# Planning a fused four-stage convolution kernel by half layers: exponentials and joins over two PSUM banks at once

## The chip, the cores and the metric

The kernel runs on one core of one Trainium2 chip. The metric is the device time of one execution in microseconds (us), the median of three. PE is TensorE, PEld its weight load, ACT ScalarE, DVE VectorE, POOL GpSimd, SP the engine that issues most DMAs. "Granted clock" is the share of TensorE's full 2.4 GHz that the throttle granted.

## The reference, cut to what matters

Input `x` is (8, 16, 128, 128) float32. Four residual stages follow each other, each on a group-normalised copy (8 groups, so 2 channels per group):

```python
x = x + _L0_conv_ref(_gn(x), ...)   # 3x3 conv, kernel mixed from 3 experts by a softmax routing of the pooled input
x = x + _L1_conv_ref(_gn(x), ...)   # abs, then depthwise 3x3
x = x + _L2_conv_ref(_gn(x), 8)     # 17 x 17 box mean, separable
x = x + _L3_conv_ref(_gn(x), ...)   # sum of 8 neighbours, then 1x1 layers:
h = elu(w1 n); h = elu(w2 h); h = elu(w3 h); h = elu(w4 h); F = w5 h   # 64 hidden channels
```

The last stage costs most: four layers of 64 x 64 products over 16,384 pixels per sample, each followed by `elu(z) = max(z, exp(min(z, 0)) - 1)`.

## The kernel before, in words

A sample lies in SBUF as 128 partitions (16 channels x 8 rows of a group of rows) x 2048 elements, cut into Q = 4 parts of 512. The first three stages (called k = 0, 1, 2) of one sample are interleaved by hand with the last stage (k = 3) of an earlier one. A round t (`one(t)`, t = 1 to 8, in each engine's block) computes the 16 layers (4 parts x 4 layers) of sample t-1's last stage, the box stage of sample t, the second convolution of sample t+1 and parts of the first one and of the statistics of samples t+1 to t+3. Before t = 1 stands a prologue. In the plan `at` = 0 to 15 counts the layers of a round, and each engine's `one(t)` says which other piece it does after which layer. Each engine runs its instructions in this order; semaphores join them.

One layer works on M = 4 PSUM banks `pz[:, m, :]` (128 x 512). Per bank (lines 785 to 801, 650 to 672, 1017 to 1043 of the kernel):

- PE (`layer`) waits for bank m of the previous layer's result (`g_written`), then multiplies: two 64 x 64 tiles, each in two float32 passes, so four matmul instructions. Even banks use the diagonal quadrants of the array, odd banks the other two, so two neighbouring banks can run at once.
- ACT (`elu`) computes `u = relu(-z)` from PSUM (L654), then `u = exp(-u)` in place (L662). It issues relu 0, relu 1, exp 0, relu 2, exp 1, relu 3, exp 2, exp 3: no exponential follows its own relu directly.
- DVE (`join`, L1025) computes `g = max(u - 1, z)`, and the next layer's matmul of that bank can go.

After a part's fourth layer PE multiplies by w5 into bank `po` (`last_layer`, L807) and DVE adds it to the sample (`output`, L1047). For the last sample, and for the first part of the one before, DVE has little else to do: there `clips` gives it banks 1 and 3, where it writes `min(z, 0)` itself (L1021) in place of ACT's relu, and ACT applies exp to that (L659); in the last sample the join of bank 3 is carried over into the next layer's time.

The other pieces that the plan places: `conv_taps` (PE, L777) 16 matmul instructions on 64 x 32 tiles for one column of taps; `box_band` (PE, L746) two instructions on the whole array, 12 bands per sample, into `pc` (`chunk_bank`); `box_scan` (DVE, L1058); `evacuate` (DVE, L1008, L1011, L1013) adds a stage's result to the sample; `chunk_stats` and `merge_stats` (DVE, L967 to L975), then `group_sums` (PE, L720), `group_var` (DVE, L982) and `scales` (POOL, L467 to L477) make a normalisation; `normal1` (ACT, L642) writes the second stage's input in two halves of 1024, `normal0` (L628 on ACT in the prologue, POOL afterwards) the first stage's, `normal2` (POOL, L525) the third's and `normal3` (DVE, L1065) the fourth's; `near_sums` (POOL) and `stacks` (DMAs, SP) prepare the fourth stage's operand, `windows0` and `windows1` (DMAs, SP) those of the first two.

Of the kernel before, what the change touches and what calls it, by code (L numbers as in the profile page):

```python
# [21 lines left out]
Q = 4  # L22
# [53 lines left out]
def build(nc, x, w_experts, conv_bias, fc_w, fc_b, w_depth, w1, w2, w3, w4, w5, con_early, con_channel, con_late, out):  # L76
    with ExitStack() as ctx:
# [122 lines left out]
        clip_done = sem("clip_done")  # L200
# [36 lines left out]
        Y0 = 8  # L237

# [9 lines left out]
        def carried(j, q):  # L248

            return isinstance(j, int) and j == B - 1 and q < Q - 1  # L250

        def steps(j, q, l, m, counted):

            n = sum(LAYERS * len(counted(i, p)) for i in range(j + 1) for p in range(Q) if (i, p) < (j, q))
            c = counted(j, q)
            return n + l * len(c) + c.index(m) + 1

        def clip_n(j, q, l, m):

            return steps(j, q, l, m, clips)  # L260

        def relu_n(j, q, l, m):

            if not isinstance(j, int):
                return zn(j, q, l, m)
            return steps(j, q, l, m, lambda i, p: [a for a in range(M) if a not in clips(i, p)])

        def elus(l):

            return g_last if l == LAYERS - 1 else g  # L270

# [78 lines left out]
        def windows1(eng, i, halves, last):  # L350

            for h in halves:
                eng.wait_ge(y1_written, 2 * i + h + 1)
                for dst, rows in around(y1, win1, h, False):
                    eng.dma_start(dst, rows).then_inc(win1_in, 16)
            if last:
                eng.wait_ge(y1_written, 2 * i + 2)
# [91 lines left out]
        def _(pool):  # L449
# [14 lines left out]
            def scales(i, k):  # L464
# [7 lines left out]
                if k < 2 and not (isinstance(i, int) and i == 0):  # L472
                    pool.wait_ge((y0_written, y1_written)[k], (Y0, 2)[k] * i)
# [82 lines left out]
            def one(t):  # L556
                if has(t + 1):
                    scales(t + 1, 1)
# [11 lines left out]
                if has(t + 3):  # L570
                    scales(t + 3, 0)
                    pool_features(t + 3)
# [24 lines left out]
            scales(3, 0)  # L597
            pool_features(3)
# [7 lines left out]
        def _(act):  # L606
# [29 lines left out]
            def normal1(i, half):  # L636
                if half == 0:
# [3 lines left out]
                rows = slice(half * K // 2, (half + 1) * K // 2)  # L641
                act.activation(y1[:, rows, 1:W + 1], sample(i).rearrange("p (k w) -> p k w", w=W)[:, rows, :], ACT.Abs,  # L642
# [7 lines left out]
            def elu(j, q, l):  # L650

                def relu(m):
# [3 lines left out]
                def exp(m):  # L656
                    if m in clips(j, q):
                        act.wait_ge(clip_done, clip_n(j, q, l, m))
                        act.activation(u[:, m, :], u[:, m, :], ACT.Exp).then_inc(exp_done, 1)  # L659
                    else:  # L660
                        act.wait_ge(relu_done, relu_n(j, q, l, m))
                        act.activation(u[:, m, :], u[:, m, :], ACT.Exp, scale=-1.0).then_inc(exp_done, 1)  # L662

                if clips(j, q):
                    relu(0)
                    exp(0)
                    exp(1)
                    relu(2)
                    exp(2)
                    exp(3)  # L670
                else:
                    relu(0)
                    for m in range(1, M):
                        relu(m)
                        exp(m - 1)
                    exp(M - 1)

            def one(t):
                first = isinstance(t, int) and t == 1
                for p in range(4):  # L680
                    for l in range(LAYERS):
                        at = 4 * p + l
                        elu(t - 1, p, l)
                        if has(t + 1):
                            if at - first in (4, 5):
                                normal1(t + 1, at - first - 4)
                        if has(t + 2):
                            if at == 5 + first:
                                softmax_exp(t + 2)
# [5 lines left out]
            normal1(0, 0)  # L695
            normal1(0, 1)
# [9 lines left out]
            normal1(1, 0)  # L706
            normal1(1, 1)
# [7 lines left out]
        def _(pe):  # L715
# [15 lines left out]
            def box_band(i, c, d):  # L731
                if d == 0:
                    if isinstance(i, int) and i == 0:
                        pe.wait_ge(conv_evac[0], Q + max(c - 1, 0))
                    elif c >= 2:
                        pe.wait_ge(conv_evac[2], Q * i + c - 1)
# [14 lines left out]
            def conv_taps(i, k, n, taps):  # L751

                if taps[0] == 0:
# [6 lines left out]
                    elif k == 1:  # L760
                        if isinstance(i, int) and i == 0:
                            pe.wait_ge(setup_dve, SETUP_DVE)
                        else:
                            pe.wait_ge(conv_evac[2], Q * i)
# [17 lines left out]
            def layer(j, q, l):  # L782
                top, bottom = slice(0, HID), slice(HID, P)
                for m in range(M):
# [20 lines left out]

# [4 lines left out]

            def one(t):
                first = isinstance(t, int) and t == 1
                for p in range(4):
                    for l in range(LAYERS):
                        at = 4 * p + l
                        layer(t - 1, p, l)
                        if l == 0 and part_before(t, p):
                            last_layer(*part_before(t, p))
                        if has(t):
                            if at == 2:  # L820
                                box_band(t, 0, 0)
                                box_band(t, 0, 1)
                            if at == 3:
                                box_band(t, 0, 2)
                                box_band(t, 1, 0)
                            if at == 4:
                                box_band(t, 1, 1)
                            if at == 5:
                                box_band(t, 1, 2)
                                box_band(t, 2, 0)  # L830
                            if at == 6:
                                box_band(t, 2, 1)
                                box_band(t, 2, 2)
                            if at == 7:
                                box_band(t, 3, 0)
                                box_band(t, 3, 1)
                            if at == 8:
                                box_band(t, 3, 2)
                        if has(t + 1):
                            if first and at < 2:  # L840
                                conv_taps(t + 1, 0, at, range(3))
                            elif at == 0:
                                conv_taps(t + 1, 0, 1, (2,))
                            if at == 9:
                                conv_taps(t + 1, 1, 0, (0, 1))
                            if at == 10:
                                conv_taps(t + 1, 1, 0, (2,))
                            if at == 11:
                                conv_taps(t + 1, 1, 1, (0, 1))
                            if at == 12:  # L850
                                conv_taps(t + 1, 1, 1, (2,))
                        if has(t + 2):
                            if at == 13:
                                conv_taps(t + 2, 0, 0, (0, 1))
                            if at == 14:
                                conv_taps(t + 2, 0, 0, (2,))
                            if at == 15:
                                conv_taps(t + 2, 0, 1, (0, 1))
                        if at == 3 + first and has(t + 1):
                            group_sums(t + 1, 1)  # L860
                        if at == 4 + first and has(t + 2):
                            logits(t + 2, (t + 1, 1))
                        if at == 9 and has(t):
                            group_sums(t, 3)
                        if at == 10 and has(t + 3):
                            group_sums(t + 3, 0)
                        if at == 14 and has(t + 1):
                            group_sums(t + 1, 2)
# [39 lines left out]
            group_sums(3, 0)  # L908
# [8 lines left out]
        def _(dve):  # L917
# [99 lines left out]
            def elu(j, q, l):  # L1017

                def clip(m):
                    dve.wait_ge(z_mm, zn(j, q, l, m))  # L1020
                    dve.tensor_scalar(u[:, m, :], pz[:, m, :], 0.0, None, ALU.min).then_inc(clip_done, 1)  # L1021

                def join(l, m, q=q):
                    dve.wait_ge(exp_done, zn(j, q, l, m))
                    dve.scalar_tensor_tensor(out=elus(l)[:, m, :], in0=u[:, m, :], scalar=-1.0, in1=pz[:, m, :],  # L1025
                                             op0=ALU.add, op1=ALU.max).then_inc(g_written, 1)

# [246 lines left out]
```

## Time and profile before

| | us |
|---|---|
| time, median of 3 runs (lowest, highest) | 763.07 (761.76, 764.73) |
| the profiled execution: its own time | 764.65 |
| its span, first to last instruction | 762.8 |
| PE busy in the span | 616.3 (81%) |
| DVE busy | 596.9 (78%) |
| ACT busy | 548.8 (72%) |
| POOL busy | 265.8 (35%) |

The span begins with about 141 us of prologue. The eight rounds follow, and about 14 us of last output and store. Busy time of an engine is the union of its instructions' durations; in a stretch of back-to-back instructions these overlap at their ends, so the distance from one start to the next (the step) is shorter than a duration. The profile was taken at a granted clock of 0.953 on average.

### The profile page before, as it was taken

How to read it: one execution, taken by the hardware profiler on the slowest of the kernel's cores; microseconds unless marked ns; L12 is line 12 of the kernel's file. 1: busy time of each engine (PE TensorE's matmuls, PEld its weight loads, DVE VectorE, ACT ScalarE, POOL GpSimd, SP SyncE). 2: the span in 40 equal slices, each digit the busy share in tenths (PEclk: the TensorE clock that was granted, in tenths of full speed). 3: DMA queues.
4: the chain of work that ended last, by engine and by line, in shares of the span. 5: the costliest groups of instructions: out<-in, count | busy, mean ns of one | idle time of the engine just before them, and what ended most of it. 6: DMA issues, size and time to landing. Idle time of an engine off the chain costs nothing.

```text
span 762.8 us, 13243 instructions
## 1 busy us (share of the span) xinstructions
PE 616.3 (81%) x4142; PEld 186.8 (24%) x4142; DVE 596.9 (78%) x1020; ACT 548.8 (72%) x1041; POOL 265.8 (35%) x431
## 2 busy tenths in 40 slices
PE   0352844789988999899989988999899789899992
PEld 0211211123223232222223322322222223222220
DVE  1242675399988998899899989878887889779993
ACT  0212110489988988898889888988898968998882
POOL 1314025407551656155624552455211620230000
PEclk9985887799999999999999999999999999999996
DMA  5749589608685858272926383646540650075002
GB/s 100 133 86 170 123 174 205 104 1 173 143 193 96 195 117 197 55 179 50 200 68 157 66 187 89 136 88 154 123 112 1 139 137 1 1 154 122 1 1 55
DMA packets 72866, 85.53 MB, mean 112 GB/s; under 512 B 8674, under 2 KB 58354, under 8 KB 72818
## 3 DMA queue, kind: packets, MB, share of 16 engines
q1 hardware_dynamic: 68096, 78.58, 47.8%
q10 hardware_dynamic: 4722, 6.34, 4.7%
q8 instruction: 26, 0.43, 0.3%
q14 instruction: 22, 0.18, 0.1%
HBM read 9.14 MB, written 8.39 MB: 23 GB/s over the span
## 4 chain that ended last, share of the span: by engine, by line
PE 33%; DVE 22%; ACT 19%; issue 10%; DMA 7%; SPq 5%; POOL 1%; ACTq 1%; DVEq 0%; POOLq 0%
PE pz L800 16%; ACT u L654 8%; ACT u L662 7%; PE pc L746 7%; PE pc L777 7%; DVE g L1025 6%; DMA win<-y 3%; DVE u L1021 3%; ACT u L659 2%; DVE bn L967 2%; DVE box_sum L1058 2%; DVE xs L1008 2%; DMA xs<-in_x_dram 2%; DVE g_last L1025 2%; SPq L375 1%
## 5 line engine op out<-in xcount | busy, mean ns | idle before, releaser
L654 ACT ACTIVATE u<-pz 128x512 f32<-128x512 f32 x472 | 275.1, 600 | 96.2 <-PE pz L800 95.4
L800 PE MATMUL pz<-g,wT 64*64 64x512 f32 x1536 | 288.1, 607 | 19.6 <-DVE g L1025 16.3
L1025 DVE SCALAR_TENSOR_TENSOR g<-u,pz 128x512 f32<-128x512 f32 x384 | 250.5, 682 | 61.7 <-ACT u L662 58.9
L662 ACT ACTIVATE u<-u 128x512 f32<-128x512 f32 x472 | 288.1, 639 | 1.3
L800 PEld LDWEIGHTS pz<-g,wT 64*64 64x64 f32 x1536 | 78.4, 131 | 206.3 <-issue 204.3
L777 PE MATMUL pc<-win,t 64*32 64x512 f32 x1392 | 95.5, 651 | 22.3 <-DMA win<-y 13.5
L746 PE MATMUL pc<-box_sum,box_mat 128*128 128x512 f32 x180 | 92.5, 631 | 12.3 <-DVE box_sum L1058 12.3
L967 DVE BATCH_NORM_STATS2 bn<-xs 128x6 f32<-128x512 f32 (+1 forms) x128 | 82.7, 681 | 19.0 <-DMA xs<-in_x_dram 17.2
L800 PE MATMUL pz<-stack,wT 64*64 64x512 f32 x512 | 83.8, 620 | 10.0 <-issue 5.5
L1025 DVE SCALAR_TENSOR_TENSOR g_last<-u,pz 128x512 f32<-128x512 f32 x128 | 82.7, 681 | 10.3 <-ACT u L662 9.1
L467 POOL TENSOR_TENSOR stat<-stat 128x1 f32<-128x1 f32 x32 | 11.1, 348 | 227.2 <-DVE stat L982 227.2
L720 PE MATMUL psm<-stat,con 128*128 128x2 f32 x64 | 12.4, 264 | 55.3 <-DVE stat L975 52.1
L642 ACT ACTIVATE y<-xs,stat 128x1024 f32<-128x1024 f32 (+1 forms) x16 | 19.9, 1258 | 44.5 <-POOL stat L477 44.5
L746 PEld LDWEIGHTS pc<-box_sum,box_mat 128*128 128x128 f32 x180 | 30.2, 189 | 73.2 <-issue 47.0
L777 PEld LDWEIGHTS pc<-win,t 64*32 64x32 f32 x1392 | 24.1, 112 | 86.4 <-issue 86.4
L1058 DVE TENSOR_TENSOR_SCAN box_sum<-y 128x580 f32<-128x580 f32 x32 | 43.1, 1354 | 1.6 <-DMA stack<-near_sum 1.6
L550 POOL TENSOR_TENSOR near_sum<-box_sum 128x512 f32<-128x512 f32 x30 | 31.8, 1060 | 36.0 <-DVE box_sum L1065 36.0
L800 PEld LDWEIGHTS pz<-stack,wT 64*64 64x64 f32 x512 | 24.2, 134 | 62.4 <-issue 60.3
L554 POOL TENSOR_TENSOR near_sum<-near_sum,box_sum 128x512 f32<-128x512 f32 x30 | 37.7, 1258 | 4.3 <-DVE near_sum L1086 2.0
L807 PE MATMUL po<-g_last,w5T 128*32 128x512 f32 x256 | 35.0, 619 | 2.8 <-DVE g_last L1025 2.8
L525 POOL TENSOR_TENSOR y<-xs,stat 128x512 f32<-128x512 f32 x20 | 20.8, 1042 | 42.4 <-DVE box_sum L1058 42.4
L659 ACT ACTIVATE u<-u 128x512 f32<-128x512 f32 x40 | 25.2, 629 | 12.2 <-DVE u L1021 12.0
(91 smaller groups left out, 413.8 us busy)
## 6 DMA issues: line engine op xcount, KB each, us to landing
stack<-near_sum SPq DMA_DIRECT2D x90, 192.0 KB, 4.0
win<-y SPq DMA_DIRECT2D x56, 260.0 KB, 4.2
win<-y SPq DMA_DIRECT2D x56, 195.0 KB, 4.3
out_dram<-xs SPq DMA_DIRECT2D x8, 1024.0 KB
stack<-box_sum SPq DMA_DIRECT2D x60, 128.0 KB, 3.9
xs<-in_x_dram SPq DMA_DIRECT2D x7, 1024.0 KB
stack<-near_sum SPq DMA_DIRECT2D x30, 128.0 KB, 2.9
win<-y ACTq DMA_DIRECT2D x8, 260.0 KB, 6.8
```

The source lines that it names most:

```text
L550: pool.tensor_tensor(o, y[:, :, 0:W], y[:, :, 1:W + 1], ALU.add).then_inc(near_pairs_done, 1)
L554: pool.tensor_tensor(o, o, y[:, :, 2:W + 2], ALU.add).then_inc(near_rows, 1)
L654: act.activation(u[:, m, :], pz[:, m, :], ACT.Relu, scale=-1.0, bias=0.0).then_inc(relu_done, 1)
L659: act.activation(u[:, m, :], u[:, m, :], ACT.Exp).then_inc(exp_done, 1)
L662: act.activation(u[:, m, :], u[:, m, :], ACT.Exp, scale=-1.0).then_inc(exp_done, 1)
L746: mm = pe.matmul(chunk_bank(i, c), box_mat[:, d, :], box_sum[:, c * KB + d:(c + 1) * KB + d, RAD:RAD + W], start=d == 0, stop=d == 2)
L777: last = pe.matmul(pair_banks(i, k, n)[2 * C * m:2 * C * m + 2 * C, h, :], mat[rows, kw, :], blocks(win[m // 2], n + 2 * h)[rows, :, kw:kw ...
L800: last = pe.matmul(pz[to, m, :], wT[rows, l, rows], src, start=True, stop=True)
L807: last = pe.matmul(po[32 * m:32 * m + 32, :], w5T[:, :], elus(LAYERS - 1)[:, m, :], start=True, stop=True)
L967: dve.bn_stats(bn[k][:, c, :], sample(i, c)).then_inc(stat_step[k], 1)
L1025: dve.scalar_tensor_tensor(out=elus(l)[:, m, :], in0=u[:, m, :], scalar=-1.0, in1=pz[:, m, :], op0=ALU.add, op1=ALU.max).then_inc(g_writte ...
L1058: dve.tensor_tensor_scan(own_rows(box_sum, c).rearrange("p k w -> p (k w)"), y2[:, c * n + BOX:(c + 1) * n + BOX], y2[:, c * n:(c + 1) * n ...
```

## The change

The unit of the plan becomes the half layer (32 slots `at` per round, `HALVES = 2 * LAYERS`), in which banks 2a and 2a+1 are worked on together. ACT does two single relus, then waits for both and does one exponential over the two banks (128 x 1024); DVE does one join over the two. `clips` and `carried` go, with DVE's `min` in the tail: all samples run alike. `normal1` comes in four pieces of 512 in place of two of 1024. The statistics' end, `group_sums`, `group_var`, `scales` and `pool_features` of sample t+2's first stage move from the end of the round before to the start of round t (POOL does them first). Box chunk 3 goes into `po` in place of `pc`, with new waits for `out_evac` before it and, for part 1, for `conv_evac[2]` before `last_layer`; `last_layer` moves off the first half layer for some parts. All other pieces are laid out anew over the 32 slots.

```diff
+        Y1 = 4
+        HALVES = 2 * LAYERS
-        def clips(j, q):
-            return (1, 3) if isinstance(j, int) and (j == B - 1 or j == B - 2 and q == 0) else ()
...
+        def pair_of(t, a):
+            return t[:, 2 * a:2 * a + 2, :].rearrange("p m n -> p (m n)")
-            return pc[:, c % 2, :]
+            return po[:, :] if c == Q - 1 else pc[:, c % 2, :]
...   (POOL, one(t))
+                if has(t + 2):
+                    scales(t + 2, 0)
+                    pool_features(t + 2)
                 if has(t + 1):
                     scales(t + 1, 1)
...
-                if has(t + 3):
-                    scales(t + 3, 0)
-                    pool_features(t + 3)
...   (ACT)
+            def normal1(i, c):
+                if c == 0:
                     act.wait_ge(norm_step[1], i * NORM + NORM)
...
+                act.activation(blocks(y1, c)[:, :, 1:W + 1], sample(i, c)..., ACT.Abs,
                                bias=st[1][:, 1:2], scale=st[1][:, 0:1]).then_inc(y1_written, 1)
+            def elu(j, q, l, a):
+                for m in (2 * a, 2 * a + 1):
                     act.wait_ge(z_mm, zn(j, q, l, m))
                     act.activation(u[:, m, :], pz[:, m, :], ACT.Relu, scale=-1.0, bias=0.0).then_inc(relu_done, 1)
+                act.wait_ge(relu_done, zn(j, q, l, 2 * a + 1))
+                act.activation(pair_of(u, a), pair_of(u, a), ACT.Exp, scale=-1.0).then_inc(exp_done, 2)
...
+                            elu(t - 1, p, l, a)
+                            if has(t + 1) and at - 3 * first in (5, 6, 7, 8):
+                                normal1(t + 1, at - 3 * first - 5)
+                            if has(t + 2) and at == 13:
                                 softmax_exp(t + 2)
...   (PE)
+            def layer(j, q, l, a):
+                for m in (2 * a, 2 * a + 1):
...
+                if q == 1 and has(j + 1):
+                    pe.wait_ge(conv_evac[2], Q * (j + 1) + Q)
...
+            box_at = {5: ((0, 0),), 6: ((0, 1),), 7: ((0, 2), (1, 0)), 8: ((1, 1),), 10: ((1, 2),), 11: ((2, 0),),
+                      12: ((2, 1),), 13: ((2, 2),), 14: ((3, 0),), 15: ((3, 1), (3, 2))}
+            last_at = {1: 0, 9: 1, 19: 2, 25: 3}
+            taps1_at = {16: (0, 0), 17: (0, 1), 18: (0, 2), 20: (1, 0), 21: (1, 1), 22: (1, 2)}
+            taps0_at = {24: (0, 0), 26: (0, 1), 27: (0, 2), 29: (1, 0), 30: (1, 1), 31: (1, 2)}
...
+                            if has(t + 2) and at == 0:
+                                group_sums(t + 2, 0, (t, 2))
+                            if has(t + 1) and at == 3 + 3 * first:
+                                group_sums(t + 1, 1)
...   (DVE)
+            def join(j, q, l, a):
+                dve.wait_ge(exp_done, zn(j, q, l, 2 * a + 1))
+                dve.scalar_tensor_tensor(out=pair_of(elus(l), a), in0=pair_of(u, a), scalar=-1.0, in1=pair_of(pz, a),
+                                         op0=ALU.add, op1=ALU.max).then_inc(g_written, 2)
+            output_at = {1: 0, 10: 1, 20: 2, 26: 3}
...
+                            if has(t + 3):
+                                if at in (17, 25, 29, 30):
+                                    chunk_stats(t + 3, 0, (17, 25, 29, 30).index(at))
+                                if at == 30:
+                                    merge_stats(t + 3, 0)
+            def near_stage(i, at):
+                if at in (3, 5, 7, 9):
+                    box_scan(i, (at - 3) // 2)
+                if at in (8, 11, 13, 15):
+                    evacuate(i, 2, (8, 11, 13, 15).index(at))
+                if at in (8, 11, 13, 16):
+                    chunk_stats(i, 3, (8, 11, 13, 16).index(at))
+                if at == 16:
+                    merge_stats(i, 3)
+                if at == 18:
+                    group_var(i, 3)
+                if at in (20, 21):
+                    normal3(i, at - 20)
+            def next_stage(i, at, first):       # the branch for t > 1
+                    if at == 0:
+                        stats_of(i, 1, (1, 3))
+                    if at == 1:
+                        merge_stats(i, 1)
+                    if at == 3:
+                        group_var(i, 1)
+                if at in (18, 22):
+                    evacuate_pair(i, 1, (at - 18) // 4)
+                if at == 19:
+                    chunk_stats(i, 2, 0)
+                if at == 23:
+                    stats_of(i, 2, (2, 1))
+                if at == 24:
+                    chunk_stats(i, 2, 3)
+                    merge_stats(i, 2)
+                if at == 26:
+                    group_var(i, 2)
+            def full_stage(i, at):
+                if at == 0:
+                    group_var(i, 0)
+                if at == 12:
+                    softmax_in(i)
+                if at == 14:
+                    route_out(i)
+                if at in (27, 31):
+                    evacuate_pair(i, 0, (at - 27) // 4)
+                if at == 28:
+                    stats_of(i, 1, (0, 2))
```

## Rows read from the trace of the kernel before

**Rows 1.** The page, parts 1 and 4: busy time, the chain that ended last.

```profile
PE 616.3 (81%) x4142; PEld 186.8 (24%) x4142; DVE 596.9 (78%) x1020; ACT 548.8 (72%) x1041; POOL 265.8 (35%) x431
PE 33%; DVE 22%; ACT 19%; issue 10%; DMA 7%; SPq 5%; POOL 1%; ACTq 1%; DVEq 0%; POOLq 0%
```

**Rows 2.** Windows by round: start:end, us, busy (x) by engine, clock, DMA, GB/s.

```profile
141.00:221.30 80.30, 75.87 (x592) 22.83 (x588) 70.36 (x120) 68.54 (x132) 34.45 (x56) 0.98 0.55 115
221.30:533.80 312.50, 289.89 (x2065) 87.83 (x2060) 278.30 (x466) 274.39 (x529) 149.28 (x227) 1.00 0.58 128
533.80:609.30 75.50, 67.74 (x432) 20.35 (x426) 64.04 (x105) 68.38 (x130) 22.25 (x31) 1.00 0.40 93
609.30:683.30 74.00, 66.16 (x316) 18.23 (x310) 59.99 (x93) 63.45 (x121) 16.81 (x21) 0.98 0.31 70
683.30:748.40 65.10, 59.65 (x282) 13.54 (x280) 62.34 (x101) 56.33 (x96) 0.00 (x0) 1.00 0.19 45
```

**Rows 3.** Waits of ACT from 200 to 600 us: engine line waited for, total us, times, longest.

```profile
ACT u L654 <- PE pz L800: 47.8, 49, 1.5
```

**Rows 4.** Groups by line and shape: xcount | busy us, mean ns | idle before, releaser.

```profile
L628 ACT ACTIVATE y<-xs,stat 128x512 f32<-128x512 f32 x12 | 9.1, 804 | 20.6 <-DMA win<-y 10.4 <-POOL stat L477 10.2
L642 ACT ACTIVATE y<-xs,stat 128x1024 f32<-128x1024 f32 x10 | 12.3, 1253 | 44.5 <-POOL stat L477 44.5
L1065 DVE TENSOR_SCALAR box_sum<-xs,stat 128x1024 f32<-128x1024 f32 x10 | 8.0, 805 | 1.9 <-POOL stat L477 1.9
L1065 DVE TENSOR_SCALAR box_sum<-xs,stat 128x1024 f32 x6 | 7.7, 1290 | 0.0
```

**Rows 5.** Timeline, start of round 3: start us, us, instruction, xcount, [idle <-releaser].

```profile
299.74 1.09 ACT L654 ACTIVATE u<-pz 128x512 f32<-128x512 f32 x2 [1.23 <-PE pz L800]
300.71 0.63 ACT L662 ACTIVATE u<-u 128x512 f32<-128x512 f32 x1
301.37 0.69 DVE L1025 SCALAR_TENSOR_TENSOR g<-u,pz 128x512 f32<-128x512 f32 x1 [0.87 <-ACT u L662]
301.49 1.09 PE L777 MATMUL pc<-win,t 64*32 64x512 f32 x16
303.74 1.18 ACT L654 ACTIVATE u<-pz 128x512 f32<-128x512 f32 x2
...
310.76 1.26 DVE L1025 SCALAR_TENSOR_TENSOR g<-u,pz 128x512 f32<-128x512 f32 x2
310.90 2.00 PE L746 MATMUL pc<-box_sum,box_mat 128*128 128x512 f32 x4 [0.70 <-DVE box_sum L1058]
...
312.82 1.95 PE L800 MATMUL pz<-g,wT 64*64 64x512 f32 x16
313.94 1.08 ACT L654 ACTIVATE u<-pz 128x512 f32<-128x512 f32 x2 [1.27 <-PE pz L800]
```

**Rows 6.** Timeline of the last round, about 742 us.

```profile
741.74 1.47 DVE L1025 SCALAR_TENSOR_TENSOR g<-u,pz 128x512 f32<-128x512 f32 x2
742.39 0.58 ACT L654 ACTIVATE u<-pz 128x512 f32<-128x512 f32 x1
743.00 0.63 ACT L662 ACTIVATE u<-u 128x512 f32<-128x512 f32 x1
743.32 0.22 PEld L800 LDWEIGHTS pz<-g,wT 64*64 64x64 f32 x4 [0.56 <-issue]
744.37 0.58 ACT L654 ACTIVATE u<-pz 128x512 f32<-128x512 f32 x1
```

**Rows 7.** Timeline of round 7, the scan of its first part.

```profile
619.03 1.37 DVE L1058 TENSOR_TENSOR_SCAN box_sum<-y 128x580 f32<-128x580 f32 x1 [1.56 <-DMA stack<-near_sum]
621.61 0.63 ACT L659 ACTIVATE u<-u 128x512 f32<-128x512 f32 x1 [2.92 <-DVE u L1021]
```

**Rows 8.** Windows in the prologue, PE's busy time against the clock (columns as rows 2).

```profile
104.00:110.00 6.00, 2.65 (x8) 1.00 (x6) 3.13 (x7) 2.37 (x2) 1.75 (x8) 1.00 0.42 95
116.00:124.00 8.00, 3.57 (x36) 1.65 (x44) 4.37 (x10) 0.00 (x0) 7.33 (x12) 0.50 1.08 197
```

More of the change, by code:

```diff
@@ L681, in one @@
                     for l in range(LAYERS):
[L682 to L688, printed above, removed]
+                        for a in range(2):
+                            at = HALVES * p + 2 * l + a
+                            elu(t - 1, p, l, a)
+                            if has(t + 1) and at - 3 * first in (5, 6, 7, 8):
+                                normal1(t + 1, at - 3 * first - 5)
+                            if has(t + 2) and at == 13:
                                 softmax_exp(t + 2)
@@ L694, in _ @@
             windows0(act, 0, (1,), False)
-            normal1(0, 0)
-            normal1(0, 1)
+            for c in range(Q):
+                normal1(0, c)
             windows1(act, 0, (1,), False)
@@ L705, in _ @@
                 normal0(2, c)
-            normal1(1, 0)
-            normal1(1, 1)
+            for c in range(Q):
+                normal1(1, c)
             act.wait_ge(conv_mm[1], 2)
@@ L839, in one @@
[L839 to L862, printed above, removed]
@@ L1164, in one @@
-                        if has(t + 3):
-                            if at == 7:
-                                chunk_stats(t + 3, 0, 0)
-                                chunk_stats(t + 3, 0, 1)
-                                chunk_stats(t + 3, 0, 2)
-                            if at == 9:
-                                chunk_stats(t + 3, 0, 3)
-                                merge_stats(t + 3, 0)
-                            if at == 12:
-                                group_var(t + 3, 0)
+                        for a in range(2):
+                            at = HALVES * p + 2 * l + a
+                            join(t - 1, p, l, a)
+                            near_stage(t, at)
+                            next_stage(t + 1, at, first)
+                            full_stage(t + 2, at)
+                            if at in output_at and part_before(t, output_at[at]):
+                                output(*part_before(t, output_at[at]))
+                            if has(t + 3):
[3 more added lines that the diff above has]
+                                    merge_stats(t + 3, 0)
@@ new lines, in near_stage @@
+            def near_stage(i, at):
+                if not has(i):
+                    return
+                if at in (3, 5, 7, 9):
[10 more added lines that the diff above has]
+                    normal3(i, at - 20)
@@ L1175, in evacuate_pair @@
+            def full_stage(i, at):
+                if not has(i):
+                    return
+                if at == 0:
[8 more added lines that the diff above has]
+                    stats_of(i, 1, (0, 2))
             def evacuate_pair(i, k, n):
@@ L1238, in _ @@
             merge_stats(3, 0)
-            group_var(3, 0)
             evacuate_pair(1, 1, 0)
```

220 lines of the change are left out of this document (45 added, 175 removed).

## The prediction

> **What bounds the kernel now.** I read the page first, then windows by round, the waits of ACT, the groups by shape, and two timelines. No engine is full: PE 81%, DVE 78%, ACT 72%, and the chain that ended last changes hands all the time (PE 33%, DVE 22%, ACT 19%) [rows 1]. Rounds 2 to 5 together take 312.5 us, 78.1 each, with PE busy for 72.5 of them, DVE 69.6 and ACT 68.6; the last round takes 65.1 [rows 2]. ACT's only long wait is for the next layer's product: 47.8 us in 400, in 49 pieces of about 1 us [rows 3]. So two things alternate. A layer with nothing beside it takes 4.0 us (its first relu starts at 299.74, the next layer's at 303.74 [rows 5]), which is eight ACT instructions at a mean of 0.50 us from start to start. A loaded layer is paced by the loop exp, join, matmul, relu with another piece in its way: there the reader is to see ACT idle 1.27 us before 313.94, after a scan on DVE (1.37 us long in [rows 7]) and four box instructions on PE (2.00) held up the joins and the products [rows 5]. The mean is 78.1 / 16 = 4.88 us a layer in a full round, 4.07 in the last.
>
> **Step 1: the new loop.** A half layer of the new plan can't start before the same half of the layer before is joined, and every instruction in it now waits for the whole of the one before. Link by link:
> - two single relus: 1.08 us (the pair at 313.94 [rows 5]);
> - the exponential now follows its own relu, which nothing did before outside the tail. A relu of 0.58 us starts at 742.39 and the exp that waits for it at 743.00, so 0.03 us between end and start [rows 6]. The drain that a back-to-back pair hides (two relus take 1.08 us, so the second starts 0.48 after the first, which lasts 0.60 [rows 5]) is in the open, 0.15 with the wait;
> - the exponential of 128 x 1024, not in the trace. One of 512 takes 0.63 [rows 5, 6]. ACT's other instruction takes 1.253 for 1024 and 0.804 for 512, 0.45 more [rows 4], which makes 1.08; from above it is two steps as now, 0.63 + 0.53 = 1.16. The 512 form of that row ran in the prologue only and reads short rows, so I put the difference a little lower and take 1.05, with 1.02 as the low end;
> - from its end to the join 0.03 us (301.34 to 301.37 [rows 5]);
> - the join of 128 x 1024, not in the trace either. From above 1.26 to 1.29: two joins back to back [rows 5], and the slow form of the DVE copy of 1024; from below that copy's fast form, 0.81 [rows 4]. A join reads two tensors, one of them in PSUM, so its own row is nearest. The 0.57 that a second join adds holds some fixed time, which one instruction pays once; I take 0.04 off, 1.22;
> - from the end of a join to the next relu: 743.21 to 744.37 is 1.16 us for one bank, of which about 0.14 until PE starts (its weights come at 743.32) [rows 6]; for two banks at once 312.82 to 313.94, 1.12 [rows 5]. Together 0.14 + 1.12 = 1.26.
>
> Sum: 1.08 + 0.03 + 1.05 + 0.03 + 1.22 + 1.26 = 4.67 us a layer. The two halves run in turn, so a slot is 2.335 us. That is more than ACT's own work: 0.48 + 0.60 + 0.03 until the exp starts and about 0.94 for its step (0.10 less than its duration) is 2.05 a slot, 4.10 a layer, and that in turn is no less than the 4.0 of now: the pairing saves a fixed part of about 0.1 per exponential and pays 0.15 for the drain in front of it. A round is at least 16 x 4.67 = 74.7 us. The bounds (exp 1.02 to 1.16, join 0.81 to 1.29) give 4.23 to 4.85.
>
> On the exponential the Trainium skill, in "ScalarE: Activation LUTs", *What ACT_TABLE_LOAD costs*, has a formula: with constant scale and bias 186 ns plus 0.833 ns per element, and about 93 ns of overlap between neighbours. Its 0.61 us for 512 stands against 0.63 here, and for 1024 it gives an estimate of 1.04 us; with that the loop would be 4.66.
>
> **Step 2: what hides beside it in a full round.** A slot leaves PE 2.335 - 1.0 (two banks dense: 16 instructions in 1.95 us for four banks [rows 5]) = 1.3 us and DVE 2.335 - 1.13 = 1.2 us. One box band (2.00 / 2) or one column of taps (1.09) fits [rows 5]; of DVE's pieces of 512, which I all take at the 0.6 us of a join's step, one fits and two nearly. So the stalls of rows 5 are gone: products no longer sit behind two bands, and PE doesn't stagger its banks. What doesn't fit:
> - normal1 on ACT: four slots (5 to 8) of 2.05 + 0.70 (0.804 less the overlap of 0.10 [rows 4]) = 2.75, 0.42 over each: 1.7 us. The two halves of now cost 2 x 1.15 us. The scales that it waits for come from `group_var` in slot 3, which lies behind a scan; POOL then has some 2 us, as now.
> - PE, slots 7 and 15: two bands, 1.0 + 2.0 = 3.0. Slot 7 hides under normal1, 15 counts 0.5.
> - DVE, slot 20: join, normal3 (1.29), output (0.60) is 3.0: 0.5 counted, as relief in the slots before takes the rest. Slots 27, 31 and 0 (pairs of evacuations or statistics, 1.4 us beside the join): 0.2 each, 0.5 in all after the light slot 30.
> - Scans (1.37 [rows 7]) and the evacuation with its statistics are 0.1 to 0.15 over in slots 3, 5, 7, 8, 9, 11 and 13. An excess after one half pushes only the other one, and two in a row of the same half cost once, so I count nothing; counted in full it is 0.8.
> - POOL's moved `scales` and `pool_features`, SP's windows and stacks: each has several slots (over 10 us) before its reader, as now; the waits for `po` (slots 14 and 19) come after the output of slot 10 and the evacuation of slot 15. Nothing; if one were late it would cost its lateness once a round.
>
> A full round: 74.7 + 1.7 + 1.5 = 77.9. That is 0.2 less than now: the half-layer plan hides nearly all the extra work, under a loop that is as long as what it hides.
>
> **Step 3: the rounds without that work.** From round 6 on there is less and less to hide, and the loop stays. Round 6 loses slots 27 and 31: 74.7 + 1.7 + 1.1 = 77.5 against 75.5 [rows 2]. Round 7 has no normal1: 74.7 + 1.1 = 75.8 against 74.0, although a stall there, in which the scan waits 1.56 us for a stack's DMAs and ACT then 2.92 us [rows 7], should go: normal3 is one or two slots earlier in the plan. The last round: 74.7 us and 0.5 for the longer last join, against 65.1 to 65.2. Without clips ACT takes back two relus a layer, but that isn't what costs: the clips let DVE and ACT share a bank's chain, and with single banks half a layer takes 1.98 us (742.39 to 744.37 [rows 6]). The pair can't go below its own chain, 4.67.
>
> **The sum.** Rounds 2 to 5: 4 x 77.9 = 311.6 against 312.5 [rows 2]: -0.9. Round 1 is 80.3 now [rows 2]; 74.7 + 1.7 + 1.7 (its evacuations crowd slots 0 to 5) + 0.5 + 1.5 (first stack) is 80.1: 0. Round 6 +2.0, round 7 +1.8, round 8 +10.0. Prologue: one `group_var` less, four pieces of normal1 in place of two on the way to the first windows, 0. Together +12.9: 764.65 of the profiled execution becomes 777.6. That execution lay 1.6 above the median of 763.07; between 776.0 and 777.6 I say 777.
>
> **The rivals.**
> - *Collisions in the full rounds* (chance 0.15). Every excess counted in full (0.8 and 1.2 more of slots 7, 20 and 27 to 0), and normal1 waiting 0.5 for its scales: 80.4 a round, 2.5 more in five rounds, 2 in round 6 and 1.5 in round 7: 777 + 16 = 793. For it: waits on a pair are longer than on one bank, so each delay holds 1024 elements. Against: phases of the halves may shift.
> - *The clock falls in the last round* (0.12). Products now come in bursts of 1.1 us every 2.335, PE busy for 47%, against 59.65 / 65.1 = 92% now, with its banks staggered [rows 2]. In the prologue the clock stayed at 2.4 GHz over a stretch with 2.65 of 6 us busy (44%) and was at 1.2 GHz in one with 3.57 of 8 (45%) [rows 8]. At 1.2 GHz a burst of 1.1 us takes about 0.85 longer (its columns take twice the time): 16 x 0.85 = 14 us, 791. The Trainium skill, "TensorE: Matmul & The Clock Gate", *A second HAM failure mode: psum-queue depth-cycling*, says that frequent short idles between groups of matmuls can make the clock swing between its two levels; the full rounds of now, with PE at 92%, show none of it.
> - *The relief wins* (0.07, the other side). Place: the full rounds; mechanism: dense PE pairs and cheap pair joins. With a loop of 4.60 and none of the heavy slots of DVE and PE showing, a full round is 73.6 + 1.7 = 75.3: -2.8 in each of four rounds, -3 in round 1, then -0.6 in rounds 6 and 7 together and +9 in the last, -6 in all: 763 - 6 = 757. It decides once a full round is under 76.4, since five of them must give back the last rounds' 8.4. With the join near its low end of 0.81 it goes to about 745, where the engines' own work would hold it. Against it: the join would have to leave its own row.
> - *It comes out even* (0.08): full rounds near 76.5, the tail as I say, 760 to 766.
>
> **How the numbers follow.** The forecast, 770 to 785, has 0.58. Slower: 0.58 + 0.15 + 0.12 = 0.85; within 0.5%, which is about what a measurement tells here, 0.08; faster 0.07. The range leaves out the faster rival, the even one and the top of the two slow ones: 767 to 792.
>
> **What would show it.** Right: exp groups of 1.05 us, joins of 1.22, layers of 4.67 in the last round with ACT idle about 0.6 a layer before its relus and released by PE, full rounds of 77 to 79, last round 74 to 76. Wrong: a last round under 72 (a link of the loop is shorter than I have it), full rounds off by over 2 us either way, ACT or DVE waiting for POOL or a DMA in each round, or a clock under 1.00 after 200 us.

## The result: 815.4 us, 6.7% slower

The changed kernel takes 815.38 us (median of 4, 814.38 to 816.6) against 763.9 of the kernel before: ratio 1.067, 95% interval 1.0625 to 1.0715. I had forecast slower, 777 us, and a range up to 792. The direction was right, the size a quarter of what came: +13 forecast, +51 measured. The time is above the range.

The profiled execution of the changed kernel took 814.6 us, span 812.8. Its page, parts 1 and 2, and the groups of the three instructions of the loop and of the relu (columns as in [rows 4]):

```profile
PE 594.2 (73%) x4142; PEld 173.5 (21%) x4142; DVE 555.1 (68%) x724; ACT 580.1 (71%) x841; POOL 261.8 (32%) x431
PEclk9975977999999999999999999999996998988765
L631 ACT ACTIVATE u<-pz 128x512 f32<-128x512 f32 x512 | 276.8, 592 | 102.5 <-PE pz L758 98.3
L633 ACT ACTIVATE u<-u 128x1024 f32<-128x1024 f32 x256 | 270.6, 1057 | 23.7 <-ACT u L631 0.4
L958 DVE SCALAR_TENSOR_TENSOR g<-u,pz 128x1024 f32<-128x1024 f32 x192 | 233.9, 1218 | 120.9 <-ACT u L633 120.0
```

Every engine is less busy than in [rows 1] except ACT, and the span is longer: the kernel waits more. The wide exponential (over two banks) takes 1.057 us and the wide join 1.218, as taken (1.05, 1.22). What is new is ACT's 23.7 us of idle time in front of the wide exponential, 0.09 for each of 256, and a clock that no longer stays up at the end. Of the 50 us between the two profiled spans, 48.5 lie in the eight rounds. Rounds 1, 2, 4, 6, 7 and 8 (columns as in [rows 2]):

```profile
141.70:225.30 83.60, 72.31 (x604) 20.12 (x604) 68.62 (x89) 70.82 (x102) 41.05 (x62) 0.99 0.60 121
225.30:308.50 83.20, 72.53 (x518) 21.59 (x516) 67.65 (x87) 71.13 (x102) 37.11 (x58) 0.98 0.66 140
389.00:468.80 79.80, 70.78 (x519) 21.41 (x517) 67.49 (x87) 71.05 (x103) 37.12 (x58) 1.00 0.54 120
548.90:631.40 82.50, 66.15 (x416) 17.59 (x414) 61.82 (x72) 70.57 (x101) 21.53 (x30) 0.92 0.43 97
631.40:711.80 80.40, 58.79 (x317) 16.29 (x314) 53.51 (x53) 68.07 (x96) 10.70 (x14) 0.94 0.28 64
711.80:797.60 85.80, 56.52 (x282) 13.05 (x280) 41.48 (x36) 67.92 (x97) 0.00 (x0) 0.75 0.06 15
```

Round 4 takes 79.8 us (78.3 before). Rounds 3 and 5 take 80.5 and 80.1, each with one fall of the clock, and round 2 takes 83.2 with one slow layer (e9 and e10 below). The last round takes 85.8 at a mean clock of 0.75, where [rows 2] had 65.1 at 1.00. The last round holds nothing but the layers, and it is the longest.

The loop itself, from the timeline of round 4, links one after another:

```profile
437.28 1.07 PE L767 MATMUL po<-g_last,w5T 128*32 128x512 f32 x8
437.34 1.09 ACT L631 ACTIVATE u<-pz 128x512 f32<-128x512 f32 x2 [0.33 <-PE pz L758]
438.48 1.29 PE L758 MATMUL pz<-g,wT 64*64 64x512 f32 x8
438.52 1.06 ACT L633 ACTIVATE u<-u 128x1024 f32<-128x1024 f32 x1
439.68 1.22 DVE L958 SCALAR_TENSOR_TENSOR g<-u,pz 128x1024 f32<-128x1024 f32 x1
441.05 1.29 PE L758 MATMUL pz<-g,wT 64*64 64x512 f32 x8 [0.21 <-DVE g L958]
```

Two relus 1.09 (437.34 to 438.43), 0.09 to the exponential, 1.06, 0.10 to the join (439.58 to 439.68), 1.22, 0.15 to PE at 441.05, and the relu of the next layer came at 442.16, 1.11 later: 4.82 us. My sum had 4.67: every link agrees to 0.01 but the two starts of a wide instruction, 0.09 and 0.10 in place of 0.03. In the second half of round 4 the layers follow each other at 4.82 to 5.02 us, whatever lies beside them (a w5 product at 437.28 here). In its first half, where the box bands, the scans and normal1 lie, most take 4.94 to 5.64.

The clock's part can be read in the last round. Two pairs of neighbouring layers, one of each at full clock and one with a fall to the lower level (0.50):

```profile
738.10:742.90 4.80, 2.39 (x18) 0.70 (x16) 3.03 (x4) 4.17 (x6) 0.00 (x0) 1.00 0.00 0
742.90:748.60 5.70, 4.34 (x18) 1.04 (x16) 2.43 (x3) 4.28 (x6) 0.00 (x0) 0.57 0.01 3
765.20:770.00 4.80, 2.28 (x16) 0.70 (x16) 2.66 (x4) 4.17 (x6) 0.00 (x0) 1.00 0.00 0
770.10:775.80 5.70, 4.18 (x17) 0.89 (x16) 2.43 (x3) 4.27 (x7) 0.00 (x0) 0.58 0.01 3
```

With the same layer to do, PE is busy 4.2 to 4.3 us in place of 2.3 to 2.4, and the layer takes 0.9 longer. Of the 16 layers of that round six take 4.82, and the ten that take 5.1 to 6.3 all have a mean clock under 1.00.

### The profile page after: what moved, and what is told of

The parts are those of the page before. It is cut to its first block, busy times and chain, and to the rows that moved or that the text cites. A ratio compares the mean times of both kernels' runs of the same rounds, so it can differ in the third digit from the quotient of the medians.

```text
span 812.8 us, 13218 instructions
## 1 busy us (share of the span) xinstructions
PE 594.2 (73%) x4142; PEld 173.5 (21%) x4142; DVE 555.1 (68%) x724; ACT 580.1 (71%) x841; POOL 261.8 (32%) x431
## 4 chain that ended last, share of the span: by engine, by line
PE 27%; ACT 23%; DVE 19%; issue 16%; DMA 5%; POOL 4%; SPq 2%; ACTq 1%; DVEq 0%; POOLq 0%
PE pz L758 16%; ACT u L631 11%; ACT u L633 10%; DVE g L958 9%; PE pc L735 4%; DMA win<-y 3%; DVE g_last L958 2%; SPq L335 2%; PE po L704 2%; DVE bn L905 2%; ACT y L619 2%; PE po L767 2%; DMA xs<-in_x_dram 2%; PE pc L704 2%; POOL y L494 2%
## 5 line engine op out<-in xcount | busy, mean ns | idle before, releaser
L758 PE MATMUL pz<-g,wT 64*64 64x512 f32 x1536 | 255.9, 659 | 85.3 <-DVE g L958 82.2
L958 DVE SCALAR_TENSOR_TENSOR g<-u,pz 128x1024 f32<-128x1024 f32 x192 | 233.9, 1218 | 120.9 <-ACT u L633 120.0
L633 ACT ACTIVATE u<-u 128x1024 f32<-128x1024 f32 x256 | 270.6, 1057 | 23.7 <-ACT u L631 0.4
L735 PE MATMUL pc<-win,t 64*32 64x512 f32 x1392 | 101.0, 657 | 29.9 <-DMA win<-y 15.6
L958 DVE SCALAR_TENSOR_TENSOR g_last<-u,pz 128x1024 f32<-128x1024 f32 x64 | 78.0, 1218 | 43.1 <-ACT u L633 42.7
L447 POOL TENSOR_TENSOR stat<-stat 128x1 f32<-128x1 f32 x32 | 6.2, 193 | 214.8 <-DVE stat L920 214.8
L704 PE MATMUL pc<-box_sum,box_mat 128*128 128x512 f32 x138 | 74.6, 635 | 0.2
L619 ACT ACTIVATE y<-xs,stat 128x512 f32<-128x512 f32 (+1 forms) x32 | 25.1, 801 | 46.6 <-POOL stat L457 46.6
L704 PEld LDWEIGHTS pc<-box_sum,box_mat 128*128 128x128 f32 x138 | 21.5, 188 | 52.4 <-issue 43.8
L496 POOL TENSOR_TENSOR y<-y,stat 128x512 f32<-128x512 f32 x28 | 29.2, 1043 | 2.2
```

Source lines behind the costliest of these rows:

```text
L619: act.activation(blocks(y1, c)[:, :, 1:W + 1], sample(i, c).rearrange("p (k w) -> p k w", w=W), ACT.Abs, bias=st[1][:, 1:2], scale=st[1][: ...
L633: act.activation(pair_of(u, a), pair_of(u, a), ACT.Exp, scale=-1.0).then_inc(exp_done, 2)
L704: mm = pe.matmul(chunk_bank(i, c), box_mat[:, d, :], box_sum[:, c * KB + d:(c + 1) * KB + d, RAD:RAD + W], start=d == 0, stop=d == 2)
L735: last = pe.matmul(pair_banks(i, k, n)[2 * C * m:2 * C * m + 2 * C, h, :], mat[rows, kw, :], blocks(win[m // 2], n + 2 * h)[rows, :, kw:kw ...
L758: last = pe.matmul(pz[to, m, :], wT[rows, l, rows], src, start=True, stop=True)
L958: dve.scalar_tensor_tensor(out=pair_of(elus(l), a), in0=pair_of(u, a), scalar=-1.0, in1=pair_of(pz, a), op0=ALU.add, op1=ALU.max).then_inc ...
```

## The experiments

Ratios are to runs of the kernel before on the same chip, with their 95% intervals. "Last round" is from its first relu to its last exponential's end; "full round" is round 4. Both are read from the one execution that was profiled.

**e1 and e2: is it the pairs, the layout, or the clips?**

```diff
# e1, on the changed kernel
-  relu, relu, wait, exp over two; join over two
+  a == 0: relu(0) relu(1) exp(0);  a == 1: relu(2) exp(1) relu(3) exp(2) exp(3);  joins of one bank
# e2, on the kernel before
-            return (1, 3) if ... else ()
+            return ()            # clips; and carried returns False
```

> The new half-layer plan as it is, but exponentials and joins over one bank each, in the order of the kernel before (relu 0, relu 1, exp 0, relu 2, exp 1, relu 3, exp 2, exp 3). No clips. Theory 1 (the chain of a pair, measured at 4.82 us a layer, sets the pace): an empty layer goes back to about 4.0 to 4.1 us, a full round to 76 to 79, the last round to 66 to 68, in all about 765 to 775. Theory 2 (the new layout of the other pieces over 32 slots costs most, the pairs little): full rounds stay near 80 and the time over 795. Theory 3 (the falls of the clock in the last rounds are a cause of their own, whatever the pairing): the last round stays over 75.

> The kernel before with the clips taken out, so that the last sample runs like the others; nothing else changed. The clips relieve ACT of 2 relus a layer. Theory 1 (the chain, not ACT's work, sets the tail): an empty layer of single banks takes 4.0 us with or without clips, so the last round goes from 65.2 to 65 to 67 us and the time from 764 to 763 to 768. Rival (the missing clips are a large part of what the last round lost): the last round goes to 70 or more, the time to 770 or more.

e1: 794.35 us, ratio 1.0442 (1.0367 to 1.0516). The last round is back at 66.3, as theory 1 has it, and the clock does not fall in it. But the full rounds take 82.3, more than with pairs, and the time lies 19 us above theory 1's range, just under theory 2's. So theory 1 holds for the tail, and the layout is bad for this order of instructions; e7 shows which of the two is at fault. e2: 761.93 us, 0.9975 (0.9942 to 1.0008). Its last round takes 65.7. Taking out the clips costs nothing, and e1 and e7 run without them too, with last rounds of 66.3 and 65.2: the missing clips are not what made the last round long.

**e4: the pairs in the old plan.**

```diff
-                    relu(0); then relu(m), exp(m - 1) for m = 1 to 3; exp(3)          # clips as in e2
+                    for a in range(2): relu(2 * a); relu(2 * a + 1); exp over banks 2a, 2a+1
-                    for m in range(M): join(l, m)
+                    for a in range(2): join over banks 2a, 2a+1
```

> The old plan by whole layers, no clips, with the exponentials and joins over two banks as in the changed kernel (relu, relu, exp over two, twice a layer). Theory 1 (the pair's chain sets the pace and the old plan's larger pieces collide with it): empty layers 4.8, full rounds 82 to 88, last round 77 or more with the clock falling, in all 815 to 850, no better than the changed kernel. Theory 2 (the new layout costs, the pairs little): 765 to 785.

842.32 us, 1.1044 (1.0976 to 1.1113): +80 over e2, which differs from it by the pairs and by ACT's order, and e8 below shows that this order costs nothing in the old plan. Full rounds 85.5. The half-layer layout takes 27 us of that back. Theory 1.

**e5, e6, e7: which pair?** All on the changed kernel, layout untouched.

```diff
# e5: joins of one bank each          # e6: two exponentials of one bank each
# e7: both, so relu(2a) relu(2a+1) exp(2a) exp(2a+1), join(2a), join(2a+1)
```

> The changed kernel with its joins over one bank each; relus and the exponential over two banks stay, and so does the layout. Theory 1 (the pair's chain): the first join of 0.68 lets bank 0 go 0.54 us earlier, the second (0.60 after it) needs about as long as before but its product overlaps; the loop is about 1.18 + 1.06 + 0.10 + 0.68 + 0.60 + 0.14 + 1.06 - 0.50 = 4.3 us a layer. Last round 69 to 71 if the clock stays up, full rounds 78 to 82, time 785 to 797. If the pair join costs nothing (rival: the exponential over two banks is what hurts), the time stays at 810 to 820.

> The changed kernel with two exponentials of one bank each, after the two relus; the join over two banks stays. Theory 1: relu, relu, exp, exp, join, product is 1.08 + 0.52 + 0.63 + 0.10 + 1.22 + 1.26 = 4.81, the same chain as with one exponential over two: 810 to 820, last round with falls of the clock. It also tells the two start gaps apart: with an exponential over one bank the gap from relu to exp is gone (hidden); if the gap from exp to join stays 0.09 to 0.10 it belongs to the wide join, if it falls to 0.03 it belonged to the wide exponential. Rival (the wide exponential with its drain is what hurts): 790 to 800.

> The changed kernel's layout with single exponentials and single joins, in the order relu, relu, exp, exp for each half layer (e1 had relu 2 between exp 0 and exp 1). Theory 1 (chains): each bank's chain is about 3.55 us, under ACT's 4.0 a layer, with 0.45 to spare, where in e1's order banks 1 and 2 had none; so full rounds shorten from 82.3 to 76 to 79, last round about 66, time 760 to 775. Theory 2 (the new layout costs by itself, in whatever order): full rounds stay at 81 to 83, time 785 to 797.

| | time us | ratio | full round | last round | its clock |
|---|---|---|---|---|---|
| changed: pair exp, pair join | 815.4 | 1.067 (1.0625-1.0715) | 79.8 | 85.8 | 0.75 |
| e6: pair join only | 801.7 | 1.047 (1.040-1.054) | 78.6 | 78.3 | 0.89 |
| e5: pair exp only | 783.3 | 1.020 (1.013-1.027) | 78.2 | 70.4 | 1.00 |
| e7: both single | 748.9 | 0.978 (0.9735-0.9821) | 74.2 | 65.2 | 1.00 |

The windows behind the last two columns of e6, e5 and e7, one row each, with up to 0.3 us more at their ends (columns as in [rows 2]):

```profile
702.30:780.60 78.30, 48.46 (x282) 12.64 (x280) 41.35 (x36) 67.49 (x128) 0.00 (x0) 0.89 0.08 19
```

```profile
687.80:758.40 70.60, 54.62 (x285) 14.30 (x280) 43.54 (x68) 66.58 (x97) 0.00 (x0) 1.00 0.14 33
```

```profile
667.90:733.40 65.50, 53.78 (x284) 13.55 (x280) 44.04 (x69) 65.26 (x130) 0.00 (x0) 1.00 0.16 39
```

The profiled executions of e5 (774.6) and e6 (797.6) were the fastest of their four, about 9 and 4 us under the median; e5's other three had a granted clock of 0.943 to 0.950 against 0.960. So the table's last three columns may flatter these two, while the times and ratios are those of all runs.

The wide join costs most: taking it out (changed to e5) gives 32 us, taking out the wide exponential (changed to e6) 14. Both together (changed to e7) give 66, more than the sum, as one wide instruction is enough to hold both banks together. The falls of the clock are in these figures. e5's layers with nothing beside them took 4.26 to 4.32 us, and 4.68 in four places with a w5 product (worked out: 4.3): bank 0 goes on while bank 1 is joined. e6 came out under its expectation (810 to 820), at 4.70 us a layer where I had 4.81: exp 0 needs only relu 0 and starts 0.11 before relu 1 has ended, which I had left out. It also had fewer falls of the clock. e7 beat its expectation too (760 to 775, full rounds of 76 to 79). It is faster than the kernel before, with the very layout of the change. So the layout is good (74.2 against 78.3 a full round), and what is slow is what it was made for. Which part of the layout gives this was not tried by itself.

In e1 only the order on ACT differs from e7: 82.3 against 74.2. Relu 2 stands before exp 1, and so exp 1 waits for whatever the layout puts on PE between banks 1 and 2. First e1, with a column of taps on PE between the halves, then e7:

```profile
437.48 1.08 ACT L631 ACTIVATE u<-pz 128x512 f32<-128x512 f32 x2 [0.30 <-PE pz L771]
437.52 1.09 PE L748 MATMUL pc<-win,t 64*32 64x512 f32 x16
438.45 0.63 ACT L635 ACTIVATE u<-u 128x512 f32<-128x512 f32 x1
438.54 1.09 PE L771 MATMUL pz<-stack,wT 64*64 64x512 f32 x8
439.67 0.60 ACT L631 ACTIVATE u<-pz 128x512 f32<-128x512 f32 x1 [0.59 <-PE pz L771]
440.16 0.62 ACT L635 ACTIVATE u<-u 128x512 f32<-128x512 f32 x1
```

```profile
420.77 1.08 ACT L631 ACTIVATE u<-pz 128x512 f32<-128x512 f32 x2
421.74 1.15 ACT L635 ACTIVATE u<-u 128x512 f32<-128x512 f32 x2
```

In e1 relu 1 has ended at 438.56 and its exponential starts at 440.16; in e7 both exponentials follow at once. PE is busy 70.99 us of e7's full round of 74.2 by its window, so with single banks the layout is near PE's own sum.

e6 and e5 also place the two start gaps. The timeline of e6, single exponentials and a wide join:

```profile
436.69 0.59 ACT L631 ACTIVATE u<-pz 128x512 f32<-128x512 f32 x1
437.17 1.15 ACT L635 ACTIVATE u<-u 128x512 f32<-128x512 f32 x2
437.42 0.69 DVE L912 BATCH_NORM_STATS2 bn<-xs 128x6 f32 x1
438.42 1.22 DVE L965 SCALAR_TENSOR_TENSOR g<-u,pz 128x1024 f32<-128x1024 f32 x1 [0.31 <-ACT u L635]
438.76 1.09 ACT L631 ACTIVATE u<-pz 128x512 f32<-128x512 f32 x2 [0.45 <-PE pz L765]
```

The exponentials follow the relus at once (436.69, 437.17: the drain is hidden), and the idle DVE starts the wide join 0.10 after their end at 438.32. The narrow join of [rows 5] started 0.03 after a narrow exponential, and e5's narrow joins start 0.03 after a wide one (the median of 140 for which DVE was idle). So each gap belongs to the wide instruction that waits. Why a wide one starts later I can't say.

**e8: ACT's new order in the old plan.**

```diff
-                    relu 0, relu 1, exp 0, relu 2, exp 1, relu 3, exp 2, exp 3        # clips as in e2
+                    relu 0, relu 1, exp 0, exp 1, relu 2, relu 3, exp 2, exp 3
```

> The kernel before, without clips, with ACT's order relu 0, relu 1, exp 0, exp 1, relu 2, relu 3, exp 2, exp 3; all single, joins as they were. By the chains bank 1 needs 0.48 + 0.52 + 0.63 + 0.03 + 0.68 + 0.14 + 1.06 = 3.54 us in place of 4.08 and bank 2 the same in place of 4.0, so that a piece of 0.4 us more fits beside each layer: full rounds 74 to 77 in place of 78.3, time 745 to 757. Rival (the loaded layers are set by PE's own sum of products, bands and taps, or by DVE's, not by the chain): 758 to 766, as before.

760.87 us, 0.9922 (0.9879 to 0.9964), full rounds unchanged at 78.3. The chain of a bank is not what sets the loaded layers of the old plan; my expectation fell and the rival stands, though whether PE's sum or DVE's sets them was not tried. The gain of e7 needs the layout and the order together. It shows in ACT's waits for products in round 4 of e8, e1 and e7:

```profile
ACT u L654 <- PE pz L800: 11.3, 11, 1.4
ACT u L631 <- PE pz L771: 11.9, 14, 1.4
ACT u L631 <- PE pz L765: 4.0, 9, 0.8
```

**e3: the clock.**

```diff
+                            if isinstance(t, int) and (t == B or t == B - 1 and at >= 20):
+                                pe.matmul(pc[:, 0, :], box_mat[:, 0, :], blocks(win1[0], 0)[:, :, 0:W], start=True, stop=True)
```

> The changed kernel with one more matmul (two passes on the whole array, about 0.9 us, into a bank that nobody reads) after each half layer of the last round, and of the last 12 half layers of the one before. It is work that the output doesn't need. Theory 1 (clock: in the last round the granted clock was 0.75 and cost 85.8 - 16 x 4.82 = 8.7 us): the clock stays at 2.4 GHz, the last round takes 77 to 78 and the time falls by 8 to 11, to 804 to 807. Rival (the chain alone, the clock beside it): the extra work changes nothing or adds 0 to 5 us.

The last round of e3 in its window:

```profile
717.70:797.00 79.30, 73.00 (x347) 19.50 (x344) 41.42 (x36) 67.77 (x96) 0.00 (x0) 1.00 0.09 22
```

With PE busy 16.5 us longer the last round is 6.5 us shorter (85.8 to 79.3), at a clock of 1.00. Together with the pairs of layers above, that shows the mechanism; its size scatters, as e10, whose last round is the changed kernel's own, took 81.8 at a clock of 0.83. By the whole time it is not shown: 810.95 us, 1.0626 (1.0553 to 1.0699), an interval that reaches the changed kernel's, and above the 804 to 807 expected. In the profiled execution 2.4 of the 6.5 us were lost again before the first round and 3.6 in rounds 1 to 7. What is left of the last round above 77.1 (16 x 4.82) is four layers of 5.4 to 5.5, where the filler and the w5 product stand together.

**e9, e10, e11: the slow layer in round 2, and the tail.** One layer of round 2 took 8.2 us in the changed kernel, 12.4 in e7. The timeline of the changed kernel, SP and PE:

```profile
240.56 6.02 SPq L376 DMA_DIRECT2D out_dram<-xs  x1
246.86 16.23 SPq L335 DMA_DIRECT2D win<-y  x10
263.13 1.36 SPq L340 DMA_DIRECT2D win<-y  x2
268.71 1.52 PE L735 MATMUL pc<-win,t 64*32 64x512 f32 x16 [2.44 <-DMA win<-y]
```

Ten window DMAs take 16.2 us to issue behind the store (the first of them 9.1), and PE, which reaches the taps in slot 16, two slots earlier than in the old plan, waits for them.

```diff
# e9 (on e7), e10 (on the changed kernel): store(t - 2) moved behind stacks(t) in SP's one(t)
# e11 (on e9), last sample only: DVE does u3 = min(z3, 0) before join 2; ACT skips relu 3
```

> The layout of the changed kernel with everything single in the order relu, relu, exp, exp per half layer (as e7), and SP's store of sample t-2 moved from the start of round t to its end, behind the windows and the stacks. In e7 one layer of the second round took 12.3 us in place of 4.1: PE waited 5.5 us for the windows of sample 3, whose twelve DMAs SP issued between 244.7 and 261.8, behind the store of 1 MB (238.3, 6.1 us) and two loads of 1 MB. Theory 1 (the store in front of them delays the windows): that layer falls to 4 to 6 us and the time from 749 to 739 to 743. Rival (the two loads alone delay them, SP being held at the last load until 237.9): the layer stays over 9 us and the time over 745.

> The changed kernel itself, with only the store moved to the end of the round. Theory 1: its slow layer in the second round (8.2 us, 3.4 over its neighbours) goes to 4.8, and the time from 815 to 811 to 812; the rest, chain and clock, stays. Rival: no change, or a change elsewhere because the store now meets the stacks of the next round (layer 0 of a round longer than 4.8).

> As e9, and in the last sample DVE takes bank 3's min(z, 0) (a clip of 0.68 us in front of the joins of the second half layer), so ACT has seven instructions a layer there in place of eight. By ACT's work a layer of the last round is 3.5 us, by the chains (3.55) about the same: theory 1, the last round falls from 66.6 to 58 to 63 and the time by 4 to 8 against e9. Rival (a clip gives nothing, as in the old plan, where leaving the clips out cost nothing: 762 against 764): the last round stays at 65 to 67.

e9: 744.37 us, 0.9747 (0.9699 to 0.9795). The layer fell from 12.4 to 8.0 only, between the two theories. The last of the twelve window DMAs was issued 10.5 us earlier than in e7 (by 251.29 against 261.75), yet PE could go on only 3.4 earlier (262.25 against 265.64). I take it that the loads in front of them hold the rest; that was not tried. It is the fastest version of this study, though its interval overlaps e7's. e10: 812.01 us, 1.059 (1.0535 to 1.0645); its slow layer went to 4.8, which is 3.3 us, within the scatter of the whole time. Some of this is not the store's: the third layer of that round took 6.2 us in place of 5.3, at a clock of 0.73, and so the windows had 0.9 us more. (The execution of e10 that was profiled was its longest, 819.4 us.) e11: 745.57 us, 0.9754 (0.9716 to 0.9793), its last round 2 us longer than e9's. The clip gives nothing: bank 3's exponential waited 0.28 us for DVE's clip at 701.3, so a clip before the joins puts DVE in the chain. The rival stands.

## Why the prediction was wrong in size

By its own steps, forecast against the profiled execution (777.6 against 814.6, 37 us):

- **Step 1, the loop: 19 us.** The mechanism was right: the tail is paced by the pair's chain, the exponential and join took what I took, the drain is open. The mis-sized term is the wait in front of a wide instruction, taken as 0.03 from narrow ones, measured 0.09 and 0.10. That is 0.13 us a layer, with roundings 0.15, and over 128 layers 19.2 us. My own bounds for the loop, 4.23 to 4.85, did hold the 4.82; the range of the time did not carry them, since 128 x (4.85 - 4.67) = 23 us on top of 777 is 800, above 792.
- **The second rival, the clock: 13 us.** I gave it 0.12 as an alternative, but the bursts that it rests on come with the forecast loop itself, so it was no alternative to it. Its price was right (0.85 us a layer, measured 5.71 - 4.82 = 0.89); its place was not only the last round. That round at 16 x 4.82 would be 77.1; it took 85.8 at a clock of 0.75, 8.7 more, of which I had 0.5. Rounds 6 and 7, at 0.92 and 0.94, are 5.4 and 3.3 above 77.1 where I had 2.8 and 1.1. In round 6 the three layers with a fall (6.08, 5.71, 5.50) are 2.8 above 4.82, in round 7 the three slow ones (5.44, 5.45, 5.47) 1.9. Only in the last round was the clock held up by an experiment (e3).
- **Step 2, what hides in a full round: 2.3 us.** Right in size: round 4 is 2.7 above 16 x 4.82, and I had 3.2 above 16 x 4.67. Rounds 2 to 5 together are 15.1 above, against 12.8. But I had costed SP's DMAs at nothing, "each has several slots"; in round 2 the windows were late, 3.3 us. The claim that the new plan takes the products from behind the bands was right, and worth more than I thought: e7 has 74.2, with 4.0 us of waits for products against 9.7 before.
- **Step 3, the tail without clips.** Right that the missing clips don't matter (e2, in the loop of single banks).
- **What is left**: 1.1 us in round 1, 0.7 before it and 0.7 behind the last round, not looked into.

19.2 + 13.0 + 2.3 + 1.1 + 1.4 = 37. *Collisions in the full rounds* did not come (2.7 above the loop in round 4, where it had 5.7). *The relief wins* was true of the layout and false of the pairs: they were one change to me, and I priced only their sum. One row was misread without effect on the sum: the layer from 299.74 to 303.74 of [rows 5] is not one with nothing beside it, as a column of taps runs in it at 301.49, and it takes 4.0 us all the same.

## What to carry to other kernels

In a dependent chain that passes from engine to engine, an instruction over two tiles saves one fixed cost on its engine (here 1.06 us against 1.15 for two exponentials, 1.22 against 1.28 for two joins) and adds the whole second tile to the latency of each link; if the engine is not full, that can be a loss (here 66 us of 815). Compare the length of the chain with the work of the busiest engine first (here 4.82 against 4.1 us), and leave the instructions narrow. A finer plan, with the pieces beside the chain cut small, is worth having with narrow instructions: the two parts of such a change are to be tried apart.

## What was not expected of the hardware

- A wide instruction (128 x 1024) that waits for a semaphore started 0.09 us (ACT) and 0.10 us (DVE) after the end of what it waited for, a narrow one (128 x 512) 0.03 on both. On DVE every profiled run shows it; on ACT a narrow exponential that waited in the open for its relu stands only in the kernel before, in its tail.
- TensorE's clock fell to 1.2 GHz again and again in a stretch where PE was busy for 56.5 of 85.8 us and idle for 0.9 us (median) between its bursts. It did not in the last rounds of the profiled e5 and e7, with 54.6 of 70.6 and 53.8 of 65.5 busy and idle times of 0.45 and 0.34. Extra matmuls held it up (e3: 73.0 of 79.3 busy, clock 1.00). The Trainium skill, "TensorE: Matmul & The Clock Gate", *A second HAM failure mode: psum-queue depth-cycling*, describes such swings from short idles between groups; this trace agrees.
